# One core, four transformer blocks: a shared place for large weights, an MLP's weights split in the attention before it, GpSimd's fills behind the tokens

## The reference, cut to what matters

```python
x = x + g_msa * _attention(_modulate(_layernorm(x), sh_msa, sc_msa), W_qkv, W_out, b_out)   # L0: 16 heads of 64
x = x + g_mlp * _ff(_modulate(_layernorm(x), sh_mlp, sc_mlp), W1, b1, W2, b2)               # W1 256x1024, W2 1024x256
...
h = film(rmsnorm(x, norm1_w), cond, film1_w, film1_b)                                       # L1: one head of 256
x = x_in + (out @ proj_w + proj_b)
h = jax.nn.gelu(h @ mlp_w1 + mlp_b1, approximate=False) @ mlp_w2 + mlp_b2
...
attn_out = _attention(x, node_mask, qkv_w, proj_w, proj_b)                                  # L2: 16 heads of 16, key mask
x = x + gate_msa[:, None, :] * _modulate(_layernorm(attn_out), shift_msa, scale_msa)
mlp_out = _mlp(x, fc1_w, fc1_b, fc2_w, fc2_b)
x = x + gate_mlp[:, None, :] * _modulate(_layernorm(mlp_out), shift_mlp, scale_mlp)
...
qkv = (h @ Wqkv.T).reshape(b, n, 3, H, HD)                                                  # L3: 16 heads of 64
y = jnp.einsum('ked,ehd->keh', g, fc1s) + b1s                                               # experts of 256x1024
```

## Time and profile before

| what | value |
|---|---|
| timed runs | 3445.57, 3440.40, 3444.59 us; median 3444.59 |
| span of the profiled execution | 3442.1 us |
| PE, PEld busy | 3093.8 us (90%), 2530.8 us (74%) |
| DVE, ACT, POOL busy | 2204.7 us (64%), 1694.4 us (49%), 804.7 us (23%) |
| mean granted TensorE clock | 0.957 of full speed |
| first up product of L0m, L1m, L2m | at 873.00, 1254.05, 1961.38 us |

### The profile page before, as it was taken

The page is one execution under the profiler, slowest core; times in us unless marked ns, Lnnn a source line. Parts: engine busy times, 40 slices in busy tenths (PEclk is TensorE's granted clock), DMA queues, the critical chain, the costliest instruction groups (busy, mean ns, idle before and its releaser), DMA issues. The chain is left out here.

```text
span 3442.1 us, 71017 instructions
## 1 busy us (share of the span) xinstructions
PE 3093.8 (90%) x26346; PEld 2530.8 (74%) x26346; DVE 2204.7 (64%) x4255; ACT 1694.4 (49%) x3085; POOL 804.7 (23%) x656
## 2 busy tenths in 40 slices
PE   7899999998898969999999699789999999994697
PEld 5777877776798969877777598567777776772686
DVE  4566656665666766667777567657575757567674
ACT  3344444443454435545555445556666666662364
POOL 1221122111112321112222211322122222221453
PEclk8999999999899989999999899899999999997798
DMA  5000000000110010010000100100000000004243
GB/s 159 10 6 6 3 6 6 6 3 7 43 24 20 0 47 0 6 44 0 0 0 0 57 19 18 29 7 0 0 0 0 0 0 0 0 1 125 84 128 71
DMA packets 64656, 80.66 MB, mean 23 GB/s; under 512 B 9666, under 2 KB 56514, under 8 KB 64308
## 3 DMA queue, kind: packets, MB, share of 16 engines
q1 hardware_dynamic: 58436, 71.13, 6.9%
q0 software_dynamic: 6144, 8.52, 1.3%
HBM read 66.80 MB, written 12.85 MB: 23 GB/s over the span
## 5 line engine op out<-in xcount | busy, mean ns | idle before, releaser
L915 POOL TENSOR_TENSOR L0a_prob<-L0a_prob 128x1024 f32<-128x1024 f32 x48 | 117.3, 2444 | 571.9 <-PE L0a_o L1270 571.9
L1017 ACT ACTIVATE L0a_prob<-L0a_st 128x512 f32<-128x512 f32 x256 | 138.7, 597 | 201.5 <-PE L0a_st L1237 174.8
L921 POOL TENSOR_TENSOR L3a_shift<-L3a_neg,L3a_mx 128x256 fp32r<-128x256 f32 x128 | 95.7, 747 | 554.4 <-DVE L3a_mx L1496 552.4
L1017 ACT ACTIVATE L3a_prob<-L3a_st 128x512 f32<-128x512 f32 x256 | 138.8, 597 | 128.5 <-PE L3a_st L1237 128.5
L1496 DVE TENSOR_REDUCE L0a_mx<-L0a_s 128x2 f32<-128x512 f32 x256 | 164.4, 684 | 39.2 <-PE L0a_s L1213 37.4
L1845 ACT ACTIVATE L2a_prob<-L2a_st 128x512 f32<-128x512 f32 x256 | 132.2, 604 | 116.1 <-PE L2a_st L1876 116.1
L1486 DVE SCALAR_TENSOR_TENSOR L3a_qk_lo<-raw,cols_sb,L3a_qk_hi 128x256 fp32r<-128x256 f32 x256 | 156.5, 651 | 36.5 <-ACT L3a_qk_hi L1008 36.5
L1496 DVE TENSOR_REDUCE L3a_mx<-L3a_s 128x2 f32<-128x512 f32 x256 | 163.8, 680 | 18.1 <-PE L3a_s L1213 18.1
L2108 DVE TENSOR_REDUCE L2a_mx<-L2a_s 128x2 fp32r<-128x512 f32 x256 | 163.5, 681 | 15.2 <-PE L2a_s L1876 15.2
L1435 DVE RECIPROCAL L0a_rsum<-L0a_sum 128x256 f32<-128x256 f32 x16 | 28.1, 1758 | 197.8 <-PE L0a_sum L1285 176.2
L1435 DVE RECIPROCAL L3a_rsum<-L3a_sum 128x256 f32<-128x256 f32 x16 | 28.1, 1758 | 174.4 <-PE L3a_sum L1285 155.4
(11 more groups left out here) (615 smaller groups left out, 11488.6 us busy)
## 6 DMA issues: line engine op xcount, KB each, us to landing
raw<-in_moe_w SPq DMA_DIRECT2D x16, 1024.0 KB, 8.6
x_sb<-in_x SPq DMA_DIRECT2D x1, 4096.0 KB, 25.1
L0a_gate<-gate_rows SPq DMA_DIRECT2D x32, 128.0 KB, 3.9
L0m_gate<-gate_rows SPq DMA_DIRECT2D x32, 128.0 KB, 3.8
L2a_gates<-gate_rows SPq DMA_DIRECT2D x2, 2048.0 KB, 9.5
L2m_gate<-gate_rows SPq DMA_DIRECT2D x32, 128.0 KB, 3.8
out_x<-x_sb SPq DMA_DIRECT2D x1, 4096.0 KB, 17.6
token_rows<-x_sb SPq DMA_DIRECT2D x1, 4096.0 KB, 29.4
```

The source lines that it names most:

```text
L915: nc.gpsimd.tensor_tensor(both[:, :, :, 0:N], both[:, :, :, 0:N], both[:, :, :, N:2 * N], ALU.add).then_inc(halves_done, 1)
L921: nc.gpsimd.tensor_tensor(shift[:, u % 4, :, :, :], neg64[:].unsqueeze(1).unsqueeze(1).to_broadcast([P, 2, TT, 64]), mx[:, u % 2, :, :].un ...
L1017: A(prob[:, u % 4, h, :], st_ps[u % 2][h][:], ACT.Exp, scale=64 ** -0.5).then_inc(p_done, 1)
```

## The change

A tile set `home` (four tiles of 2048 elements per partition) lives for the whole program. L0a's and L3a's large weights, the three MLPs' weights and the experts' weights use it in turn. `split_weights` is gone. `home_weights` gives SP, ScalarE and VectorE one instruction for each of four pieces, and the attention before an MLP calls them: L0a and L2a in the last batch, L1a in the last two, each at a fixed place between the other instructions. In L0a SP loads the first two pieces after the last q and k product, in L1a all four at the start, in L2a three at the start. The MLP no longer waits for weights. L2a's gate rows are loaded for one batch at a time, after the last update of the previous batch. In an MLP with `ahead`, GpSimd waits for `xn_done` to reach 2 before `ahead[1]`, which in L1m moves the fills behind the second iteration's scalings.

```diff
+def home_weights(nc, t, g, nm, stage):
...
+    def sync_share(sp, n):
+        src, to, _, _, _ = pieces[n]
+        if n >= slots:
+            sp.wait_ge(lo_done, 4 * turn + n - slots + 1)
+        sp.dma_start(to, src).then_inc(landed[n], 16)
+    def scalar_share(act, n):
+        _, _, raw, hi, _ = pieces[n]
+        act.wait_ge(landed[n], 16 * (turn + 1))
+        nc.scalar.activation(hi, raw, ACT.Copy).then_inc(hi_done, 1)
+    def vector_share(dve, n):
+        _, _, raw, hi, lo = pieces[n]
+        dve.wait_ge(hi_done, 4 * turn + n + 1)
+        nc.vector.tensor_tensor(lo, raw, hi.bitcast(F32), ALU.subtract).then_inc(lo_done, 1)
+        if n == 3:
+            dve.wait_ge(lo_done, 4 * turn + 4)
...
@@ head256 (L1a), scalar @@
+                if not more:
+                    weights[1](act, 3)
                 if more:
                     qk_hi(i + 1, 1)
                 if more2:
                     x_hi(i + 2, False)
+                elif more:
+                    weights[1](act, 0)
+                    weights[1](act, 1)
                 act.wait_ge(pv_done, i + 1)
                 A(o[0][:].rearrange("p c n -> p (c n)"), o_ps[:], ACT.Copy).then_inc(ohi_done, 1)
+                if more and not more2:
+                    weights[1](act, 2)
...
@@ head256 (L1a), vector @@
+                if not more:
+                    weights[2](dve, 2)
                 if more:
                     qk_low(i + 1, 1)
                 if more2:
                     modulate(i + 2, False)
+                elif more:
+                    weights[2](dve, 0)
+                    weights[2](dve, 1)
...
                 o_low(i)
+                if not more:
+                    weights[2](dve, 3)
...
@@ heads64 (L0a), sync, scalar, vector @@
+                sp.wait_ge(qk_done, U * B)
+                weights[0](sp, 0)
+                weights[0](sp, 1)
+                sp.wait_ge(ep_done, B - 1)
...
+                    if gated and final:
+                        for n in {0: (0,), 1: (1,), 3: (2, 3)}.get(p, ()):
+                            weights[1](act, n)
...
+                    if gated and final:
+                        for n in {1: (0,), 2: (1,), 3: (2, 3)}.get(p, ()):
+                            weights[2](dve, n)
...
@@ heads16 (L2a) @@
-                sp.dma_start(gates[:, j, :, :], t["gate_rows"][at + j, :, :].partition_broadcast(P)).then_inc(gate_in, 16)
+                sp.dma_start(gates[:, j, :], t["gate_rows"][at + j, 0, :].partition_broadcast(P)).then_inc(gate_in, 16)
+            for n in range(3):
+                weights[0](sp, n)
             clear_used(sp, g)
+            with sp.Fori(0, B - 2) as i:
+                sp.wait_ge(y_step, 3 * i + 3)
+                for j in range(2):
+                    sp.dma_start(gates[:, j, :], t["gate_rows"][at + j, bass.ds(i + 1, 1), :].squeeze(0).partition_broadcast(P)).then_inc(gate_in, 16)
+            weights[0](sp, 3)
...
-                gated_wait(gate_in, 32)
+                gated_wait(gate_in, 32 * j + 32)
...
+                    if final:
+                        weights[1](act, u)
...
+                    if final:
+                        weights[2](dve, u)
...
@@ mlp @@
-            loader(sp=sp)[0]()
...
             if ahead:
+                gated_wait(xn_done, 2)
                 ahead[1](pool)
...
-            loader(act=act)[1]()
-            pe.wait_ge(lo_done, KD)
-                pe.wait_ge(lo_done, len(pieces))
-            loader(dve=dve)[2]()
```

More of the change, by code:

```diff
@@ L355, in head256 @@
         cols = g["cols"]
+        weights = home_weights(nc, t, g, "L1m", sb("w_stage", [P, 4, 1024])[:])
         w_in = [sem(f"w_in_{n}") for n in names]
@@ L2180, in mlp @@
             [pb(f"down{j}") for j in range(T4)]
-        w1 = [sb(f"w1{j}", [P, KD, MLP], F32R) for j in range(2)]
-        w2 = [sb(f"w2{j}", [P, MC, D], F32R) for j in range(2)]
-        stage = sb("stage", [P, 2, 1024])
+        w1, w2 = home_chunks(g["home"], 0), home_rows(g["home"], 2)
         xn, xm = sb("xn", [P, T4, D]), sb("xm", [P, KD, NN])
@@ L3097, in program @@
         early_out = sem("early_out")
+        g.update(home=[sb(f"home{j}", [P, 2048], F32R) for j in range(4)], home_in=[sem(f"home_in{n}") for n in range(4)],
+                 home_hi=sem("home_hi"), home_lo=sem("home_lo"))
         conditioning(nc, t, g)
```

94 lines of the change are left out of this document (38 added, 56 removed).

## The result

The changed kernel takes **3419.55 us** (median of four timed runs, 3419.02 to 3420.56), the kernel before beside it 3445.08 (3440.40 to 3447.58): a ratio of 0.9929, 95% interval 0.9915 to 0.9943, or 25.5 us less. The predicted time was 3426, its range 3413 to 3439. The span of the profiled execution went from 3442.1 to 3417.4 us, 24.7 less, and I account for that.

A forecast was written before the change was run, and what follows sets the result against it. TensorE, the busiest engine, was taken to bound the kernel where it stands still or runs at its lower clock. Terms -12.05 - 19.2 + 4.7 + 0.6 + 6.9 = -19.0 took 3444.6 to 3426 us; own range 3416 to 3435, with rivals 3413 to 3439.

The forecast's parts named there:

- Fills behind the tokens: L1m's first iteration: with GpSimd's fills after the scalings, statistics come 23.50 us apart as in L0m, not 35.55; -12.05 us.
- Starts: Starts of the three MLPs: first product 2.3 us earlier each, and the stop after two chunks goes; together -19.2 us.
- the model of two chunks at the lower clock and three at the upper: MLP starts: without the stop, the fifth Gelu comes 9.1 us after the first product; -5.3 in L1m, -4.3 in L0m.
- its stop and the bias add alone: L2m's start: the stop of 1.68 us goes, -1.7, and the bias add comes earlier, -1.0.
- Tail of L0a: L0a's last batch: first split held behind GpSimd's pair sum, maxima slip 3.2 us, later splits push the reciprocals; +4.7 us.
- The second part, +1.4 at the reciprocal: L0a's last batch: the last two splits meet the next pair sum and gate add, pushing the reciprocals about 1.4 us.
- Tail of L1a: L1a's last batches: copies fit into ScalarE's waits, second split pushes the low part of o by half a split; +0.6 us.
- Tail of L2a: L2a's last batch: splits delay maxima (1.0, then 2.9) and reciprocals (2.0), a fallen clock costs 1; +6.9 us.
- Gates: L2a: per-batch gate loads move GpSimd's add back about 3.8 us, covered by its wait for the variance; 0.
- Fills that hold subtractions: Rival, L1m: L2420's subtractions held about 10 us beside the fills, TensorE too; +12, 3438 us; chance 0.12.
- Last batches that swallow the work: Rival, last batches of L0a, L1a, L2a: copies and splits hide, tails cost 0 to 2; 3414 us; chance 0.11.
- The reload that becomes a wait: Rival, L2a: GpSimd's late add holds VectorE about 2 us in each of 15 batches; +30, 3456 us; chance 0.06.

The follow-up runs named there:

- fills_read: The changed kernel with three of GpSimd's zero fills (wq[1], wk[0], wk[1]) made as copies of a zeroed tile: 3418.03 us, ratio 0.9937.
- gates_only: The kernel before with only L2a's gates reloaded per batch, two loads of 128 KB: 3442.82 us, ratio 0.9999.
- after_fills_back: The changed kernel without GpSimd's wait for xn_done, so the fills start right behind its first bias add again: 3432.73 us, ratio 0.9972.
- fills_only: The kernel before with one line more, GpSimd's wait for xn_done 2 ahead of its fills: 3431.55 us, ratio 0.9971.
- after_again: The changed kernel itself, timed again on another chip as the mark for three other runs: 3422.02 us, ratio 0.9936.
- l2a_gaps: The changed kernel with the four splits of L2a's last batch put where VectorE and ScalarE wait: 3414.30 us, ratio 0.9913.
- both_gaps: The kernel of l2a_gaps with the splits of L0a's last batch moved as well: 3413.36 us, ratio 0.9909.

## Why the prediction was right, point by point

**Fills behind the tokens, -12.05.** Right in sign, size and reason. The trace gives -12.1, the wait alone 11.4 by the medians. Setting this term by a row of statistics beside a fill rather than by the add of the earlier trace rows was right: fills_read shows that the same bytes with a source would have held them, if by 0.4 to 0.7 us each. The reason was incomplete in one thing. I wrote that the scalings stand still as long as GpSimd goes on without a gap. The traces of before and gates_only bear that out, since the first scaling ends at GpSimd's first gap; in four profiled executions of after_fills_back's kernel all four scalings were through after 7 us, under GpSimd's first fills. The price of 12 us is that of the longer stall. That the medians of fills_only agree with it speaks for the long stall in most runs of the kernel before.

**Starts, -19.2.** The trace gives -2.5 three times, -3.3, -5.5 and -4.1, together -20.3. The -5.5 of L1m is partly luck: the 14.40 us that I started from were long for this code, and the forecast took over the same excess. The first product followed the tokens at once (2.3 forecast, 2.45 measured), and the model of two chunks at the lower clock and three at the upper (9.1 us) met L1m (8.93) and L2m (9.08); its own terms, 2 x 2.56 + 3 x 1.28, make 8.96. It missed two sizes in opposite directions. L0m took 10.06, since its clock rose 6.4 us after its first product and L1m's after 3.8 (a product takes 0.40 us instead of 0.63 from 877.69 and from 1249.77 on); in after_again L0m took 8.46, so this is chance between executions. For L2m I had credited its stop and the bias add alone (-1.7 - 1.0), where -4.1 came: I should have used the same 9.1 there, against the 13.21 us that its own rows gave.

**Tail of L0a, +4.7.** This is the step that failed, though the sum held: "The split reads two SBUF operands, so as in the earlier trace rows it is held to 829.8 and ends at 831.0". I took from one row that VectorE is always the one that waits. Here GpSimd was: the split was done after 1.22 us, the first maxima slipped by 0.8 us instead of 2.8, and the last by 1.1. What they lost came through the pair sum, which ended 1.05 us later and on which the shift and TensorE's next sum waited. The second part, +1.4 at the reciprocal, came as 1.1, and 0.6 came back from the reciprocal to L0m's start, where I had half a microsecond for a fallen clock; more of the output product ran at the upper level (a product takes 0.28 us instead of 0.41 from 853.66 on, 31.3 us behind the mark, and from 854.39 before, 31.1 behind it).

**Tail of L1a, +0.6.** +0.4: the low part of o is pushed by 0.3 us and the rest hides.

**Tail of L2a, +6.9.** Right in mechanism; that the sum is met to 0.1 is luck. The first split cost 1.5 (1.0 forecast). The second cost 2.7 (2.9): the maxima slipped 3.5 more, but 0.8 of that had been lost before its copy, as `L2a_o_raw` comes 2.3 us later than before against the mark, behind products that take 1.93 us at the lower clock and 1.07 at full speed. Another 1.7 were lost up to the take, 1.25 of them in the output product, which ran largely at the lower clock. The fourth split cost 1.0 at the reciprocal (2.0), and 0.8 were won back at the end. So the fallen clock cost some 2 us where I had one, and the splits less at the reciprocal. l2a_gaps shows that it was the place and not the work.

**Gates, 0.** gates_only has it by itself: 0.9999. The add moved back by less than forecast, 0.7 us in the loop in the mean where I had 3.8; only the last two batches have the full wait.

**The rivals.** Fills that hold subtractions: refuted by the 0.69 us of both traces with the wait. Last batches that swallow the work: not so here (tails of 8.8 in sum), but true of other places in the same batches, since both_gaps has L0a's tail at 36.69 us and L2a's at 42.92, where the traces without splits have 36.07 to 36.38 and 40.25 to 42.08. The reload that becomes a wait: refuted. The result lies between the forecast and the rival of swallowed tails; of the 5.7 us by which the two spans differ more than forecast, 3.1 are the tail of L0a, 1.1 the starts and 1.1 L3a.

**What stays open.** L3a, which got addresses of the home and nothing else, took 947.4 us in both traces of the kernel after, 947.4 to 948.9 in all with a home, 948.5 to 949.9 in the three without. Whether that is the addresses or chance no run was made for. And why a scaling gets in between two fills in some executions, for 7 us in all, and only at the first gap in others, for 16, is not explained.

## What to carry to other kernels

In these traces a memset on GpSimd is free beside VectorE's subtractions, statistics and scalings out of PSUM and costly beside its scalings from SBUF to SBUF; ask of each GpSimd run of work what VectorE does under it, and order it by a semaphore rather than by hope. Work that is moved from the start of a phase into the tail of the one before is only hidden where its engine waits: read the last batch's idle times in the timeline, and put it behind the instructions that others wait for, not in front of them. When two engines exclude each other, cost both orders, and follow what waits for the loser. And read a stretch in more than one profile of the same code before its length becomes the base of a forecast.
